# GNN layer kernel, phase B: register loads of eight offsets, no filler products, and row one-hots of two groups in four read back from HBM

## The chip, the cores and the metric

One core of one Trainium2 chip. The metric is the device time of the whole program in microseconds, the median of several runs.

## The reference

Three layers of an attention graph network over 12,500 nodes and 200,000 edges (64 channels), then a residual sum and a layer norm. Cut to what matters:

```python
for l in range(3):
    f1 = relu(x[row] @ nb_W[l] + nb_b[l])
    f2 = relu(x[col] @ self_W[l] + self_b[l])
    h = relu(concatenate([f1, f2], axis=1) @ att1_W[l] + att1_b[l])
    log_alpha = (h @ att2_W[l] + att2_b[l])[:, 0]
    mask = clip(sigmoid(log_alpha) * 1.5 - 0.45, 0.0, 1.0)
    rowsum = segment_sum(mask, row) + 1e-06
    d = clip(rowsum ** (-0.5), 0.0, 10.0)
    vals = mask * d[row] * d[col]
    x = segment_sum(vals[:, None] * x[col], row)
    out = out + x
return layernorm(x_in + out)
```

## The kernel before

Once, at the start, the edges are sorted by the block of 128 nodes that their row lies in, and cut into 1,664 tiles of 128 edges. Eight tiles (U = 8) are a **group**, four groups a **quad**: 208 groups and 52 quads in each layer. Then each layer has three parts: the products over nodes, phase A (the attention mask of every edge, and the sums of the mask over rows), and phase B (the weighted sum of the neighbours' rows).

**Phase A** runs the loop over quads. GpSimd (POOL) gathers the neighbours' rows with 32 indirect DMAs a quad (line 491). VectorE (DVE) makes for each group a one-hot of the edges' rows twice (`hot_a`, `hot_b`, lines 1014 to 1018). The DMA queue of SyncE (SP) stores the gathered rows of groups 0, 1 and 2 of a quad to HBM (`kept_x`), and one-hots over the columns (`look_hot`).

**Phase B** goes over the same quads in its own order. Groups 0, 1 and 2 of a quad are steps 0, 1 and 2, and group 3, whose rows POOL gathers again (line 504), is summed inside step 1. A step works like this:

- TensorE (PE) in `pick_rows` looks up d of the columns for the step after next: 24 bf16 products (line 650) from `look_t` (`onehot_t` in the trace), which SP loads.
- DVE in `look_up` takes the one value that matters of each, eight instructions (line 1078), builds the row one-hot of the next step in f32 with `build_onehot` (line 891), adds the last step's bank to `acc` in `join` (line 1093), and multiplies d with the mask in `weigh` (line 1086).
- ScalarE (ACT) in `scale_rows` multiplies the step's rows by these weights, eight instructions (line 790), and signals after the fourth and the eighth.
- PE clears the step's bank with a product of zeros (line 655) and then in `sum_edges` adds eight f32 products of one-hot and rows (line 517; the trace shows two records for each). Where in the bank a product goes is an offset that is known only at run time. The eight offsets of a group, three bits each, are packed in one 32-bit word of `spots_of`; PE's sequencer loads four such words at the end of a quad (line 663), and cuts an offset out with a shift and a mask ahead of each product.

Behind each step's work PE issues two more products of zeros into bank 7, which nobody reads (`stay_busy(2)`). So a quad has ten products of zeros: four that clear, six that do not.

In the trace the steps are told apart by tile names, since some buffers lie in the space of others: `bank<-k_x,k_hot` is step 0, `bank<-k_x,p_all` step 1, `bank<-onehots,g_hot` group 3, `bank<-p_all,onehots` step 2. PE works through its program in order; its sequencer (PEq) runs ahead of the array where nothing stops it. DVE and ACT are in order as well. The waits on the way of a step: `k_wt` (weights ready, ACT waits), `k_xs` (half of the rows scaled, PE waits), `k_w` (one-hot ready, PE waits), `k_rows` (products of `pick_rows` ready, DVE and SP wait), `k_o` (sums done, DVE and SP wait), `k_acc` (bank free, PE waits). SP issues for each step the load of `look_t` for the step after next and the load of `k_x`.

## Time and profile before

| | us |
|---|---|
| median of 3 runs | 9556.0 (9550.26 to 9559.7) |
| the profiled execution | 9558.15 |
| its span, first to last instruction | 9556.3 |
| phase B, 3 layers (windows 2764:3577, 5728:6540, 8673:9500) | 2452 |

The profile's page gives for each engine the time that it was busy, and for 40 equal slices of the span the busy share in tenths, with the clock that TensorE was granted (10 tenths would be 2.4 GHz, 5 is 1.2 GHz; a 9 stands for 90% or more). Phase B is where PEclk shows 9. The timeline gives instructions in order of time: start, duration, engine, line, operation, output and inputs, count, and in brackets the idle time of the engine before them. Matmuls overlap, so a step of PE is read from start to start. `issue` as releaser means that the profile shows nothing that the engine waited for.

### The profile page before, as it was taken

To read this page: it belongs to the slowest core of one execution; us is meant where nothing else is said; L and a number is where in the kernel's file an instruction comes from. 1 tells how busy PE (TensorE), PEld (TensorE's weight loads), DVE (VectorE), ACT (ScalarE), POOL (GpSimd) and SP (SyncE) were. 2 spreads that over 40 slices of the span, in tenths; PEclk is the share of its full clock that TensorE was granted. 3 is DMA by queue.
4 is the path that set the end of the run, shared out by engine and by line. 5 is a ranking of instruction groups with operands and counts; after the bars stand their busy time and mean duration, and the time that the engine had idled before them with its cause. 6 is when DMAs were issued, how large, how long until landed. Compare 5 with 4: busy or idle time off the path is not lost.

```text
span 9556.3 us, 210132 instructions
## 1 busy us (share of the span) xinstructions
PE 6162.0 (64%) x44565; PEld 5447.6 (57%) x44566; DVE 7276.2 (76%) x29518; ACT 3239.7 (34%) x8192; POOL 6097.4 (64%) x6294
## 2 busy tenths in 40 slices
PE   3145555555569996555555559998555555557997
PEld 1135555555568885555555548887555555556886
DVE  8877777777778887777777778887777777777888
ACT  0022222222235553222222225554222222224554
POOL 0027777777765556777777765555777777775553
PEclk7565555555569996555555559997555555557998
DMA  1014444444454444444444454444444444445443
GB/s 23 0 60 112 111 112 112 112 112 112 112 123 120 119 109 124 111 112 112 112 111 111 111 122 117 120 118 116 111 111 111 111 111 112 112 111 126 119 120 97
DMA packets 986887, 1025.83 MB, mean 107 GB/s; under 512 B 633540, under 2 KB 637412, under 8 KB 986852
## 3 DMA queue, kind: packets, MB, share of 16 engines
q1 hardware_dynamic: 787172, 657.03, 23.2%
q0 software_dynamic: 199680, 368.45, 18.0%
q14 instruction: 28, 0.23, 0.0%
q8 instruction: 7, 0.11, 0.0%
HBM read 744.64 MB, written 280.29 MB: 107 GB/s over the span
## 4 chain that ended last, share of the span: by engine, by line
PE 35%; POOL 23%; issue 20%; DVE 13%; DMA 5%; ACT 3%; ACTq 0%; DVEq 0%; POOLq 0%; SPq 0%
PE bank L517 17%; POOL k_hot L491 10%; POOL g_hot L491 9%; PE bank L650 6%; PE bank L618 6%; DMA k_hot<-qx_table,index 5%; POOL got L491 4%; PE bank L655 3%; DVE acc L903 2%; DVE acc L904 2%; ACT k_x L760 2%; PE bank L608 1%; DVE bank L1034 1%; DVE hidden L1036 1%; DVE small L1039 1%
## 5 line engine op out<-in xcount | busy, mean ns | idle before, releaser
L618 PE MATMUL bank<-p_all,onehot_t 128*128 x10032 | 2301.5, 424 | 1686.5 <-issue 1672.7
L618 PEld LDWEIGHTS bank<-p_all,onehot_t 128*128 128x128 f32 x10032 | 2186.8, 330 | 1737.7 <-issue 1737.7
L491 POOL DMA_INDIRECT got<-qx_table,index x2496 | 2372.0, 950 | 784.3 <-issue 739.5
L504 POOL DMA_INDIRECT got<-y_table,index x1248 | 1330.8, 1066 | 1087.5 <-ACT index L806 658.9
L770 ACT ACTIVATE small<-small 128x8 f32<-128x8 f32 x624 | 130.2, 209 | 3853.6 <-DVE small L1041 3781.4
L491 POOL DMA_INDIRECT k_hot<-qx_table,index x1248 | 1178.0, 944 | 393.5 <-issue 376.0
L491 POOL DMA_INDIRECT g_hot<-qx_table,index x1248 | 1185.4, 950 | 380.4 <-issue 379.2
L517 PE MATMUL bank<-mask,onehots 128*128 128x3 bf16 x4992 | 671.2, 184 | 1041.1 <-DVE mask L1052 1041.1
L517 PEld LDWEIGHTS bank<-mask,onehots 128*128 128x128 bf16 x4992 | 517.4, 104 | 1305.9 <-issue 1200.7
L1078 DVE SCALAR_TENSOR_TENSOR p_all<-iota_b,col_hi,bank 128x104 f32<-128x104 bf16 x3768 | 956.2, 317 | 327.3 <-PE bank L650 322.9
L790 ACT ACTIVATE k_x<-k_x,k_weight 128x64 f32<-128x64 f32 x2496 | 630.0, 334 | 1038.9 <-DVE k_weight L1086 993.4
L1018 DVE TENSOR_SCALAR onehots<-iota_b,rows_now 128x128 bf16<-128x128 bf16 x5040 | 945.6, 280 | 22.4
L1018 DVE TENSOR_SCALAR onehots<-iota_b,rows_b 128x128 bf16<-128x128 bf16 x5016 | 885.5, 272 | 22.0
L755 ACT CAST onehot_t<-bank 128x1024 f32<-128x1024 bf16 x630 | 637.6, 1012 | 524.2 <-PE bank L608 514.7
L1034 DVE TENSOR_TENSOR bank<-bank,got 128x512 f32<-128x512 f32 x312 | 218.2, 699 | 608.9 <-DMA got<-qx_table,index 603.7
L608 PE MATMUL bank<-ident_b,onehots 128*128 128x128 bf16 x5040 | 667.7, 314 | 9.1 <-DVE onehots L1018 9.1
L650 PE MATMUL bank<-d,onehot_t 128*128 128x104 bf16 x11376 | 616.2, 212 | 56.0 <-issue 30.5
L608 PEld LDWEIGHTS bank<-ident_b,onehots 128*128 128x128 bf16 x5040 | 631.7, 164 | 10.3 <-DVE onehots L1018 10.3
L650 PEld LDWEIGHTS bank<-d,onehot_t 128*128 128x128 bf16 x11376 | 546.9, 99 | 80.8 <-issue 61.1
L1036 DVE SCALAR_TENSOR_TENSOR hidden<-bank,a_cur 128x512 f32<-128x512 f32 x624 | 431.3, 691 | 21.4
L655 PE MATMUL bank<-zeros_b 128*128 128x512 bf16 x1563 | 446.2, 384 | 0.0
L1039 DVE TENSOR_REDUCE small<-hidden 128x8 f32<-128x512 f32 x624 | 428.0, 686 | 21.2
(170 smaller groups left out, 9724.3 us busy)
## 6 DMA issues: line engine op xcount, KB each, us to landing
onehot_t<-look_hot SPq DMA_DIRECT2D x474, 256.0 KB, 3.0
k_x<-col_rows SPq DMA_DIRECT2D x318, 256.0 KB
kept_x<-got SPq DMA_DIRECT2D x312, 256.0 KB, 3.2
look_hot<-k_x SPq DMA_DIRECT2D x312, 256.0 KB, 2.1
k_x<-kept_x SPq DMA_DIRECT2D x312, 256.0 KB
look_new<-col_rows SPq DMA_DIRECT2D x156, 256.0 KB
got<-qx_table,index POOLq DMA_INDIRECT x2496
kept_x<-g_hot SPq DMA_DIRECT2D x156, 256.0 KB
```

The lines of the kernel that those rows point to most:

```text
L491: pool.indirect_dma_start(got[j][:, k, :], None, qx_table, bass.IndirectOffsetOnAxis(ap=index[j][:, k:k + 1], axis=0)).then_inc(a_got[j], 16)
L504: pool.indirect_dma_start(got[j][:, k, 0:HID], None, y_table, bass.IndirectOffsetOnAxis(ap=index[j][:, k:k + 1], axis=0)).then_inc(g_got[j ...
L517: return mm(to, lhsT, rhs, start=False, stop=True, skip_group_check=True)
L608: last = turn(bank_t[:, k, :], hot_a[j][:, k, :], ident_b[:, :])
L618: last = mm(bank_p[h][:, k, :], onehot_t[h][:, k, :], p_all[:, ds(ids[k], 1), :].rearrange("p o d -> p (o d)"), start=True, stop=True)
L650: last = mm(bank_d[n % 3][:, e, 0:NB], look_t[i % 3][:, q * (U // 2) + e, :], d3[:, s, :], start=(s == 0), stop=(s == 2))
L655: return mm(to[:, :], zeros_b[:, 0:PARTS], zeros_b[:, :], start=True, stop=True, skip_group_check=True)
L755: a.copy(onehot_t[h][:, :, :], bank_t).then_inc(a_trc, 1)
L790: last = a.activation(to[:, k, 0:HID], rows[:, k, 0:HID], ACT.Copy, scale=by(k))
L1018: last = v.tensor_scalar(to[:, k, :], iota_b[:, :], rows[:, k:k + 1], None, ALU.is_equal)
L1036: link(v.scalar_tensor_tensor(out=hidden[h][:, :, :], in0=bank_p[h], scalar=0.0, in1=a2_cur[:, :].unsqueeze(1).to_broadcast([PARTS, U, HID ...
L1078: last = v.scalar_tensor_tensor(out=picked[:, e, :], in0=iota_b[:, 0:NB], scalar=col_hi[:, ds(at + e, 1)], in1=bank_d[(2 * i + q) % 3][:, ...
```

## The change

Four edits, three of them in phase B:

1. **Offsets.** `spots_of` is gone. PE loads the eight 32-bit offsets of one group straight from `spot_of` (`load_spots`), right behind the sums of the group before. In the product the offset is the register times 64, and shift and mask are gone. The products of the group that comes next use the registers: group order 0, 1, 3, 2 of a quad.
2. **Products of zeros.** `stay_busy` is gone: only the four clearing ones of a quad are left. A bank is cleared before the wait for the one-hot, as before.
3. **Row one-hots of groups 0 and 2 of a quad.** In phase A these lie in `hot_b[0]` in bf16. SP now stores them to HBM (`row_hot`, 256 KB each, two a quad), and DVE waits for that store to land before it overwrites `hot_b[0]`. In phase B SP loads them back (`load_hot`, two a quad, into `hot_in`), and ACT turns them into f32 (`cast_hot`, 128x1024) where DVE built them before. `cast_hot` waits for the load and for the sums that last read `k_hot`. DVE builds only the one-hots of step 1 and of group 3.
4. **Small things.** Two more stores of zeros at the start, one wait of POOL at the start of a layer, and eight small DVE instructions less when the offsets are made.

```diff
@@ (DRAM, SBUF)
+        row_hot = nc.dram_tensor("row_hot", ((2 * QUADS + 1) * PARTS, U * PARTS), BF16, kind="Internal").ap()
...
-        spot_of = sb("spot_of", [1, TILES], I32)
-        spots_of = sb("spots_of", [1, GROUPS + 4], I32)
+        spot_of = sb("spot_of", [1, TILES + U], I32)
...
+        hot_in = {0: look_new[2], 2: sb("hot_in2", [PARTS, U * PARTS], BF16)[:, :]}
...
+        def hot_there(l, quad, i):
+            return l * (QUADS + (i % 3 == 0)) + (quad + (i // 3 + 1))
@@ sync, phase A
                     for j in range(3):
                         load_columns(b, j + 2)
+                        if j != 1:
+                            sp.wait_ge(a_hotb, l * (GROUPS + 1) + (b * 4 + (j + 1)))
+                            sp.sem_inc(sp_go, 1)
+                            sp.dma_start(row_hot[ds((b * 2 + j // 2) * PARTS, PARTS), :],
+                                         hot_b[0].rearrange("p k m -> p (k m)")).then_inc(a_hotst, 16)
                         sp.wait_ge(a_got[j], (l * QUADS + b + 1) * GOT)
@@ sync, phase B
+                def load_hot(b, i):
+                    c = i % 3
+                    if not isinstance(b, int):
+                        sp.wait_ge(k_cast[c], hot_there(l, b, i - 3))
+                        sp.sem_inc(sp_go, 1)
+                    sp.dma_start(hot_in[c], row_hot[ds((b * 2 + (2 * (i // 3) + c // 2)) * PARTS, PARTS), :]).then_inc(k_hotin[c], 16)
...
                         load_look(b * 2, i + 2)
+                        if i % 3 != 2:
+                            load_hot(b * 2, i + 2)
                         sp.wait_ge(*summed(l, b * 2, i - 3))
@@ gpsimd, start of a layer
+                pool.wait_ge(k_cast[0], l * (QUADS + 1))
+                pool.sem_inc(pool_go, 1)
@@ tensor, phase B
-                def stay_busy(n):
-                    for _ in range(n):
-                        clear(bank[7])
-                def spots(b):
-                    pe.load(spot, spots_of[0:1, ds(b * 4, 4)])
-                def sum_edges(to, j, hot, rows, ready, half):
-                    of = pe.snap(spot[j], min_val=0, max_val=(1 << 3 * U) - 1)
-                    to_left = HID.bit_length() - 1
+                def load_spots(g):
+                    pe.load(spot, spot_of[0:1, ds(g * U, U)])
+                def sum_edges(to, hot, rows, there, ready, half, after):
+                    clear(to)
+                    pe.wait_ge(*there)
                     for k in range(U):
-                        bits = of >> (3 * k - to_left) if 3 * k > to_left else of << (to_left - 3 * k) if 3 * k < to_left else of
-                        at = pe.snap(bits & ((U - 1) * HID), min_val=0, max_val=(U - 1) * HID)
+                        at = pe.snap(spot[k], min_val=0, max_val=U - 1)
                         if k % (U // 2) == 0:
                             pe.wait_ge(ready, half + (k // (U // 2) + 1))
-                        last = plus(to[:, ds(at, HID)], hot[:, k, :], rows[:, k, 0:HID])
+                        last = plus(to[:, ds(at * HID, HID)], hot[:, k, :], rows[:, k, 0:HID])
+                    load_spots(after)
...
                         pe.wait_ge(*joined(l, b, i - 3))
-                        clear(bank[i])
-                        pe.wait_ge(k_w, l * (K_STEPS + 1) + k + 1)
-                        sum_edges(bank[i], i, k_hot[i], k_x[i], k_xs, (l * K_STEPS + k) * 2).then_inc(k_o[i], 1)
-                        if i == 2:
-                            spots(b + 1)
+                        there = (k_cast[i], hot_there(l, b, i)) if i != 1 else (k_w, l * QUADS + (b + 1))
+                        sum_edges(bank[i], k_hot[i], k_x[i], there, k_xs, (l * K_STEPS + k) * 2,
+                                  b * 4 + (1, 3, 4)[i]).then_inc(k_o[i], 1)
                         pick_rows(b, i + 2)
                         if i == 1:
                             pe.wait_ge(g_acc, m)
-                            clear(bank[3])
-                            pe.wait_ge(g_w, m + 1)
-                            sum_edges(bank[3], 3, g_hot, g_x, g_xs, m * 2).then_inc(g_o, 1)
-                        stay_busy(2)
+                            sum_edges(bank[3], g_hot, g_x, (g_w, m + 1), g_xs, m * 2, b * 4 + 2).then_inc(g_o, 1)
@@ scalar, phase B
+                def cast_hot(b, i):
+                    act.wait_ge(k_hotin[i % 3], hot_there(l, b, i) * 16)
+                    if not isinstance(b, int):
+                        act.wait_ge(*summed(l, b, i - 3))
+                    a.copy(k_hot[i % 3].rearrange("p k m -> p (k m)"), hot_in[i % 3]).then_inc(k_cast[i % 3], 1)
...
                         scale_rows(k_x[i % 3], k_x[i % 3], lambda k: k_weight[i % 2][:, 1, k:k + 1], k_xs)
+                        if i % 3 == 2:
+                            cast_hot(b * 2, i + 1)
                         if i % 3 != 1:
                             continue
...
                         a.copy(index[j][:, :], col_id[:, ds((b * 8 + (4 * j + 11)) * U, U)]).then_inc(g_idx[j], 1)
+                        cast_hot(b * 2, i + 1)
@@ vector, phase A (build_hot of hot_b[0])
                     dve.wait_ge(*free)
+                    if stored is not None:
+                        dve.wait_ge(a_hotst, stored * 16)
@@ vector, phase B
-                build_onehot(k_hot[0], row_lo[:, 0:U]).then_inc(k_w, 1)
...
                         look_up(i + 1, k + 1, next_at)
-                        build_onehot(k_hot[(i + 1) % 3], row_lo[:, ds(next_at, U)]).then_inc(k_w, 1)
+                        if i % 3 == 0:
+                            build_onehot(k_hot[1], row_lo[:, ds(next_at, U)]).then_inc(k_w, 1)
```

How the rows of PE stand in its program, first before, at the end of the sums of group 3 and the start of those of step 2 (`bank<-p_all,onehots`; rows named L655 are the products of zeros, REGISTER_ALU and ISA are register instructions of the sequencer, some of which carry a wait):

```order
L517 REGISTER_ALU x2
L517 ISA
L517 MATMUL bank<-onehots,g_hot 128x64
L655 MATMUL bank<-zeros_b 128x512 x2
L685 REGISTER_ALU
L655 MATMUL bank<-zeros_b 128x512
L687 ISA
L666 ISA
L517 REGISTER_ALU x2
L517 ISA
L517 MATMUL bank<-p_all,onehots 128x64
```

The same place after the change:

```order
L698 ISA
L550 MATMUL bank<-onehots,g_hot 128x64
L691 ISA
L691 TENSOR_LOAD spot_of
L688 MATMUL bank<-zeros_b 128x512
L698 ISA
L550 ISA
L550 MATMUL bank<-p_all,onehots 128x64
L698 ISA
L550 MATMUL bank<-p_all,onehots 128x64
```

Two of three products of zeros are gone, a load of registers stands between the last product of one group and the first of the next, and one register instruction is left ahead of a product where there were three.

ACT in phase B before, behind the scaling of group 3's rows, until the second step 0 of the loop's body:

```order
L806 ISA
L806 COPY index<-col_id 128x8
L797 REGISTER_ALU
L790 ACTIVATE p_all<-p_all,k_weight 128x64 x8
L796 ISA
L797 REGISTER_ALU
L790 ACTIVATE k_x<-k_x,k_weight 128x64 x8
```

And after:

```order
L846 ISA
L846 COPY index<-col_id 128x8
L824 REGISTER_ALU
L825 CAST onehots<-hot_in 128x1024
L835 REGISTER_ALU
L816 ACTIVATE p_all<-p_all,k_weight 128x64 x8
L822 ISA
L825 CAST k_hot<-look_new 128x1024
L834 ISA
L835 REGISTER_ALU
L816 ACTIVATE k_x<-k_x,k_weight 128x64 x8
```

A cast now stands ahead of the scaling of step 2 and one behind it, ahead of the scaling of step 0.

## Rows read from the trace of the kernel before

**Rows 1.** The page: busy time of the engines, and the granted clock in 40 slices.

```profile
PE 6162.0 (64%) x44565; PEld 5447.6 (57%) x44566; DVE 7276.2 (76%) x29518; ACT 3239.7 (34%) x8192; POOL 6097.4 (64%) x6294
...
PEclk7565555555569996555555559997555555557998
```

**Rows 2.** Lines, 1000:2700 (phase A), POOL: count | busy us, mean ns | idle before.

```profile
L491 POOL DMA_INDIRECT got<-qx_table,index x673 | 636.8, 946 | 205.1 <-issue 192.3 <-ACT index L779 12.8
```

**Rows 3.** Timeline of one quad of phase B: start us, us, what.

```profile
3242.31 2.67 PE L517 MATMUL bank<-k_x,p_all 128*128 128x64 f32 x16 [0.24 <-issue]
...
3244.81 1.27 PE L650 MATMUL bank<-d,onehot_t 128*128 128x104 bf16 x24
...
3245.92 0.38 PE L655 MATMUL bank<-zeros_b 128*128 128x512 bf16 x1
...
3246.14 2.11 PE L517 MATMUL bank<-onehots,g_hot 128*128 128x64 f32 x16
...
3248.09 0.81 PE L655 MATMUL bank<-zeros_b 128*128 128x512 bf16 x3
...
3248.73 2.44 PE L517 MATMUL bank<-p_all,onehots 128*128 128x64 f32 x16
...
3251.36 1.27 PE L650 MATMUL bank<-d,onehot_t 128*128 128x104 bf16 x24 [0.19 <-issue]
3252.34 0.32 DVE L1078 SCALAR_TENSOR_TENSOR p_all<-iota_b,col_hi,bank 128x104 f32<-128x104 bf16 x1 [1.93 <-PE bank L650]
...
3254.30 1.22 DVE L891 TENSOR_TENSOR p_all<-iota_b,row_lo 128x1024 f32<-128x1024 bf16 x1
...
3255.43 0.68 DVE L1093 TENSOR_TENSOR acc<-acc,bank 128x512 f32 x1
...
3256.22 2.02 ACT L790 ACTIVATE k_x<-k_x,k_weight 128x64 f32<-128x64 f32 x8 [4.53 <-DVE k_weight L1086]
...
3257.62 2.62 PE L517 MATMUL bank<-k_x,p_all 128*128 128x64 f32 x16 [0.19 <-issue]
```

**Rows 4.** Timeline of PE, start of the first phase B: clock 0.5, then 1.0.

```profile
2770.49 3.67 PE L517 MATMUL bank<-k_x,k_hot 128*128 128x64 f32 x16 [4.19 <-ACT k_x L790]
2773.95 2.29 PE L650 MATMUL bank<-d,onehot_t 128*128 128x104 bf16 x24
2776.03 1.48 PE L655 MATMUL bank<-zeros_b 128*128 128x512 bf16 x3
2777.31 1.98 PE L517 MATMUL bank<-k_x,p_all 128*128 128x64 f32 x16
2779.13 1.26 PE L650 MATMUL bank<-d,onehot_t 128*128 128x104 bf16 x24
```

**Rows 5.** Register loads of PE by line: count, duration ns min/median/max.

```profile
L663 PEldq TENSOR_LOAD <-spots_of x159: 328/332/761, 2764.3 to 9496.7; - x159
...
L613 PEldq TENSOR_LOAD <-block_of x627: 1917/1922/2570, 673.8 to 8665.5; - x157
```

**Rows 6.** Page, a cast by ACT; POOL in 3000:3500; a DMA of 256 KB.

```profile
L755 ACT CAST onehot_t<-bank 128x1024 f32<-128x1024 bf16 x630 | 637.6, 1012 | 524.2 <-PE bank L608 514.7
...
L504 POOL DMA_INDIRECT got<-y_table,index x263 | 280.3, 1066 | 225.0 <-ACT index L806 151.1 <-issue 74.0
...
onehot_t<-look_hot SPq DMA_DIRECT2D x474, 256.0 KB, 3.0
```

**Rows 7.** Timeline of PE where the clock fell, and where it did not.

```profile
3549.85 2.75 PE L517 MATMUL bank<-k_x,p_all 128*128 128x64 f32 x16 [0.51 <-ACT k_x L790]
3552.39 2.29 PE L650 MATMUL bank<-d,onehot_t 128*128 128x104 bf16 x24
...
9488.02 2.62 PE L517 MATMUL bank<-k_x,p_all 128*128 128x64 f32 x16 [0.19 <-issue]
9490.52 1.27 PE L650 MATMUL bank<-d,onehot_t 128*128 128x104 bf16 x24
```

**Rows 8.** Windows: busy us (instructions) of PE PEld DVE ACT POOL, clock, DMA share, GB/s.

```profile
3552.00:3556.00 4.00, 4.00 (x36) 3.90 (x36) 3.64 (x20) 2.49 (x11) 0.00 (x0) 0.57 0.14 34
```

More of the change, by code:

```diff
@@ L964, in _ @@
             spots = spot_of[0:1, 0:TILES].rearrange("p (t k) -> p t k", k=U)
-            link(v.tensor_tensor(spots, by_step, by_step[:, :, 0:1].to_broadcast(steps_wide), ALU.subtract))
-            v.memset(spots_of[0:1, GROUPS:GROUPS + 4], 0)
-            packed = spots_of[0:1, 0:GROUPS].unsqueeze(2)
-            link(v.tensor_copy(packed, spots[:, :, U - 1:U]))
-            for k in reversed(range(U - 1)):
-                last = v.scalar_tensor_tensor(out=packed, in0=packed, scalar=8.0, in1=spots[:, :, k:k + 1],
-                                              op0=ALU.mult, op1=ALU.add)
-                if k:
-                    link(last)
-            last.then_inc(s_edges, 1)
+            v.memset(spot_of[0:1, TILES:TILES + U], 0)
+            v.tensor_tensor(spots, by_step, by_step[:, :, 0:1].to_broadcast(steps_wide), ALU.subtract).then_inc(s_edges, 1)
             dve.wait_ge(s_edges, 1)
```

28 lines of the change are left out of this document (20 added, 8 removed).

## The prediction

> **What bounds the kernel now.** I read the page first: DVE is busy for 76% of the span, PE and POOL for 64%, and no engine is at its limit over the whole [rows 1]. The clock line splits the program: PEclk is 5 for long stretches (phase A) and 9 in three short ones (phase B) [rows 1]. So each stage needs its own reading.
>
> In phase A POOL gathers without a break: one gather is 946 ns of work and some 0.3 us of idle time ahead of it (205.1 us over 673), which is 1.25 us [rows 2]. 32 of them make 40 us a quad, 52 quads 2.08 ms, and three layers 6.2 ms of the 9.56. PE, DVE and ACT wait for gathers there.
>
> In phase B PE is busy all the time, and nearly each row of PE in the timeline follows the last with no idle time [rows 3]. A quad is the stretch from the sums of step 1 to the same sums one quad later, 3242.31 to 3257.62, 15.3 us. 156 such quads are 2.39 ms, nearly all of phase B. The reader is to follow one loop through it, in which each piece starts when the last ends: sums of step 1 2.50, `pick_rows` 1.11, a product of zeros 0.22, sums of group 3 1.95, three products of zeros 0.64, sums of step 2 2.63 (0.19 of it idle), the first half of `pick_rows` and the way to DVE 0.98, eight look-ups 1.96, a one-hot 1.13, join and weights 0.79, scaling until PE starts 1.40. That is 15.31 us [rows 3]. Step 0 of PE lies beside it.
>
> **The change, part by part.**
>
> *Sums.* The sixteen records of one `sum_edges` take 2.50 us from start to start where PE's sequencer works through shift, mask and address ahead of each product [rows 3], and 1.82 us (2777.31 to 2779.13) at the same clock right after a slow stretch, when products had piled up ahead of the array [rows 4]. The difference of 0.68 us is the price of the register instructions, and with one of three left the sequencer is no longer the slower of the two. In the loop are the sums of step 1 (2.50 to 1.82), of group 3 (1.95 to 1.82) and of step 2 (2.44 to 1.82): 1.43 us less. From the fourth scaled row to the first product 1.40 us pass, of which two of three register instructions go: 0.2 us less.
>
> *Products of zeros.* In the loop three stand behind group 3, and one is left: 0.64 to 0.22, 0.42 us less. The others (two behind step 0, two behind step 2) lie beside DVE's part of the loop and are worth nothing here; the clock is their other side, below.
>
> *The load of eight offsets.* The trace has two register loads: four 32-bit words in 332 ns, and eight 16-bit numbers in 1922 ns [rows 5]. The bounds for eight 32-bit words are 0.33 us (as for four) and 1.92 us. I take 0.45 us, near the 332 ns, since type and tensor are the same as there; twice 332 is 0.66. It blocks the sequencer, not the array, and products already handed over cover it: with two of three register instructions gone, the sequencer needs for 1.82 us of array work at most half of its 2.50 us. Where the wait for the second half of the rows ends late (2.02 us of scaling [rows 3]) the cover is thinner. For three loads in the loop I take 0.4 us exposed in all, against the 0.19 us of idle time behind step 2 now: 0.2 us more. At 0.66 us each it is 0.6 us more on top, 100 us of the total.
>
> *One-hots from HBM.* DVE loses two of four one-hots, 2.27 us a quad, but not the one that stands in the loop (3254.30, step 1's) [rows 3]. DVE waits 1.93 us in a quad already [rows 3], so these two only widen a gap: worth nothing to this loop. ACT gets two casts. The same shape out of PSUM takes 1.01 us [rows 6]. ACT works 4 x 2.02 + 0.18 us a quad and waits for the rest, so 10.3 us of 13.7 is no bound. But one cast stands ahead of the scaling of step 2, and the sums of step 2 wait for it. There PE has pick, clear and sums of group 3 to do, which covers the cast. SP gets two more loads of 256 KB, and its queue has for each a wait on a cast, behind which the loads of `k_x` and of the next `look_t` stand. They land some 3 us after issue [rows 6] and are needed a step or more later: nothing, as long as that holds.
>
> *Phase A.* Two stores of 256 KB a quad, with one wait each on SP, and a wait of DVE for the landing before `hot_b[0]` is used again, two groups (some 20 us) later. Behind SP's wait stand the stores of `kept_x`. POOL sets the pace, with indices ready about a group ahead: 0, at most 10 us in all (the first and last quads of a layer).
>
> *The sum.* 1.43 + 0.2 + 0.42 - 0.2 = 1.85 us less by these rows. I take off 0.2 us for what becomes late next (the waits between the engines that now show, DVE's own register loads behind a missing one-hot): 1.65 us a quad, 13.7 us instead of 15.3. Times 156 it is 257 us. Against the profiled execution's 9558 us that gives 9301, and 9299 against the median, 2 us below.
>
> **The clock.** With the clock at 1.2 GHz the sums of a group take 3.46 us (2770.49 to 2773.95) and `pick_rows` 2.08 [rows 4], so each group costs 1.64 and each pick 0.97 us more than at 2.4 GHz. Phase B keeps the high clock almost without a break, but at 3549.85 PE idled 0.51 us, did the sums of step 1, and the `pick_rows` behind them ran at the low clock: 2.29 us instead of 1.27, mean clock 0.57 in that stretch [rows 7, 8]. With an idle time of 0.19 us in the same place, at 9488.02, it did not fall [rows 7]. It came back within 4 us, with pick and three products of zeros close together at the start of a phase [rows 4].
>
> After the change PE has less to do in a quad, and I expect about 0.9 us of idle time ahead of the sums of step 1: from the sums of step 2 to those of step 1 the loop takes 8.0 us by the sum above, and PE's work in it is 2 x (1.82 + 1.11 + 0.22) = 6.3 us and some 0.8 for loads and the loop's end (an allowance). That is more idle time than what let the clock fall once, and the six products that kept PE busy are gone. That a fall needs the right moment is my reading of the rows (0.51 us is seen with a fall, 0.19 without). I take one fall in ten quads, 16 in all, a guess. One lasts longer than before, since no three products of zeros follow a pick; a whole quad at the low clock costs 3 x 1.64 + 1.5 x 0.97 + 0.4 = 6.8 us in the loop, and I take 5 us for a fall. 16 x 5 = 80 us.
>
> The Trainium skill (TensorE: Matmul & The Clock Gate, "Loop structure matters more than you think") holds that matmuls back to back keep the engine warm and that it is a long wait between them which lets it go cold. By that alone no idle time of a microsecond would matter, and the time would be the 9299 of the first rival. The trace speaks against it with the fall behind 0.51 us.
>
> **Forecast:** 9556 - 257 + 80 = 9379, say 9380 us; as a case 9340 to 9450. Chance 0.45.
>
> **Rivals.**
>
> *The clock holds throughout.* Then the 80 us stay: 9300 us, 9285 to 9340. For it speaks that sums get denser as well, and that a quad of 13.7 us may meet no bad moment. Chance 0.25.
>
> *The clock falls often.* The place is the idle time ahead of the sums of step 1; the price 5 us a fall; it decides from 257 / 5 = 51 falls, one in three quads. In every second quad it is 78 falls: 9556 - 257 + 390 = 9689 us, slower than before. For it speaks that the idle time comes back in each quad and that a cold stretch needs PE to be packed densely to end, for which the filler products served. Chance 0.15, the half of it on the slower side (9450 to 9750).
>
> *The load costs as much as the one of `block_of`*, 1.92 us [rows 5]. Each of three in the loop is then 1.47 us longer than I took: 4.4 us, less the 1.65 gained, is 2.75 us a quad, 429 us, or 9985 us. It decides from 0.45 + 1.65 / 3 = 1.0 us a load. Against it speak the 332 ns for the same tensor type. Chance 0.05.
>
> The Trainium skill (Runtime: NRT & Kernel Launch, "Instruction fetch mechanics") puts such a load at about 200 ns a register, even in bulk. For eight that would be an estimate of 1.6 us, which agrees with the 1922 ns for eight 16-bit numbers and not with the 332 ns for four 32-bit words. By it the last rival would come out, somewhat milder.
>
> *The gain goes elsewhere.* The casts, SP's queue with its new waits, or the loads of `k_x` under 30% more traffic become the loop, and it stays at 15 us and more: 9520 to 9570 us. Against it: POOL's eight gathers take 8 x (1.07 + 0.3) = 10.9 us a quad and it waits 4.6 for ACT (151.1 us in 33 quads) [rows 6]; ACT (10.3 us) and DVE (15.3 - 1.93 - 2.27 = 11.1 us) have room too. Chance 0.10.
>
> **How the numbers follow.** A measurement of this kernel tells 0.2%, 19 us, from no change. Faster by more: 0.45 + 0.25, 0.05 of the often-falling clock, 0.02 of the last: 0.77. Within: 0.02 and 0.07: 0.09. Slower: 0.08 + 0.05 + 0.01: 0.14. The range for 8 in 10 is 9285 to 9560; left out are the slower cases, and a little below.
>
> **What would show it.** In the changed profile: sixteen records of sums in 1.8 to 2.0 us; a register load of `spot_of` near 0.45 us; a quad of 13.7 us where the clock is 1.0; DVE's waits for PE longer than 1.93 us; phase A unchanged at 1.25 us a gather. The mean clock in phase B tells the first cases apart: near 1.0 now, about 0.95 by the forecast, under 0.85 where falls eat the gain. Wrong it would be with a load over 1 us, a quad over 14.5 us at full clock, or POOL with waits in phase A.

## The result, and the profile after

The changed kernel takes 9282.7 us (median of 4, 9279.9 to 9284.6) against 9555.7 for the kernel before: 0.971 of its time (95% interval 0.970 to 0.973). That is 273 us less, where 176 were forecast, and 2 us below the low end of the range. The profiled execution took 9279.89 us.

The page of the changed kernel:

```profile
PE 5731.3 (62%) x43629; PEld 5187.9 (56%) x43630; DVE 6885.6 (74%) x29195; ACT 3520.0 (38%) x8507; POOL 6079.3 (66%) x6294
...
PEclk7565555555559996555555558998555555556998
```

The pattern of [rows 1] is there again, with slightly shorter stretches of 9. Phase A's gathers, in 1000:2700, POOL (columns as in [rows 2]):

```profile
L524 POOL DMA_INDIRECT got<-qx_table,index x677 | 639.6, 945 | 206.3 <-issue 205.4 <-ACT index L805 0.9
```

945 ns of work and 0.3 us of idle time ahead, as in [rows 2]: the two stores per quad cost nothing there. From the first to the last gather, the three phases A took 2084, 2086 and 2087 us, before 2088, 2089 and 2089. From the first to the last sums, phase B took 716, 716 and 715 us, before 804, 805 and 803. So 265 us of the gain lie in phase B and 9 in phase A.

One quad of phase B in the timeline, PE only, to be laid beside [rows 3] (L550 the sums, L683 `pick_rows`, L688 a product of zeros):

```profile
3223.78 2.06 PE L550 MATMUL bank<-k_x,p_all 128*128 128x64 f32 x16 [0.81 <-ACT k_x L816]
3226.21 1.27 PE L683 MATMUL bank<-d,onehot_t 128*128 128x104 bf16 x24 [0.37 <-issue]
3227.32 0.38 PE L688 MATMUL bank<-zeros_b 128*128 128x512 bf16 x1
3227.53 1.90 PE L550 MATMUL bank<-onehots,g_hot 128*128 128x64 f32 x16
3229.27 0.38 PE L688 MATMUL bank<-zeros_b 128*128 128x512 bf16 x1
3229.48 1.89 PE L550 MATMUL bank<-p_all,onehots 128*128 128x64 f32 x16
3231.21 1.26 PE L683 MATMUL bank<-d,onehot_t 128*128 128x104 bf16 x24
...
3237.29 2.06 PE L550 MATMUL bank<-k_x,p_all 128*128 128x64 f32 x16 [0.64 <-ACT k_x L816]
```

And DVE and ACT in the part of the loop that is theirs, first DVE and then ACT:

```profile
3232.20 0.32 DVE L1116 SCALAR_TENSOR_TENSOR p_all<-iota_b,col_hi,bank 128x104 f32<-128x104 bf16 x1 [1.14 <-PE bank L683]
...
3234.16 1.22 DVE L932 TENSOR_TENSOR p_all<-iota_b,row_lo 128x1024 f32<-128x1024 bf16 x1
3235.30 0.68 DVE L1131 TENSOR_TENSOR acc<-acc,bank 128x512 f32 x1
```

```profile
3236.08 2.02 ACT L816 ACTIVATE k_x<-k_x,k_weight 128x64 f32<-128x64 f32 x8 [2.57 <-DVE k_weight L1124]
```

Read from start to start, the same chain as in [rows 3] closes after 13.51 us:

| piece | before | after |
|---|---|---|
| sums of step 1, its load | 2.50 | 2.43 |
| pick_rows | 1.11 | 1.11 |
| product of zeros | 0.22 | 0.21 |
| sums of group 3, its load | 1.95 | 1.74 |
| products of zeros | 0.64 | 0.21 |
| sums of step 2, its load | 2.63 | 1.73 |
| half of pick, way to DVE | 0.98 | 0.99 |
| look-ups | 1.96 | 1.96 |
| one-hot | 1.13 | 1.14 |
| join, weights | 0.79 | 0.78 |
| scaling, until PE starts | 1.40 | 1.21 |
| **quad** | 15.31 | 13.51 |

The 2.43 us of step 1 are 2.06 of sums and 0.37 in which PE is idle behind them and the profile names only `issue`: its sequencer is loading registers. The load, by line (count, ns min/median/max):

```profile
L691 PEldq TENSOR_LOAD <-spot_of x627: 587/591/1722, 2756.0 to 9217.9; - x157
```

What the engines waited for in 3000:3400 (us in total, times, longest):

```profile
POOL got L537 <- ACT index L846: 81.3, 27, 4.7
...
DVE p_all L1116 <- PE bank L683: 63.2, 59, 1.9
...
ACT k_x L816 <- DMA k_x<-kept_x: 31.9, 29, 1.6
...
DVE acc L1131 <- issue: 13.0, 27, 0.5
```

ACT now waits for a load of `k_x` once a quad, which it did not before. That is step 0's scaling, which lies beside the loop (0.81 us of slack ahead of the sums of step 1 are left). The windows of the same stretch show the clock (columns as in [rows 8]):

```profile
3000.00:3400.00 400.00, 357.35 (x4115) 332.08 (x4112) 323.22 (x1673) 286.98 (x1022) 251.16 (x236) 0.98 0.57 174
```

Over the whole trace I counted quads (starts of the sums of step 1) by the granted clock in them. Before: 148 of 153 quads inside the phases at 1.0 throughout, 15.37 us each. After: 128 at 1.0 throughout, 13.50 us each, and 25 that touch a stretch at 0.5, 15.17 us each; there are 20 such falls. One of them, where PE idled ahead of step 1:

```profile
3304.82 2.06 PE L550 MATMUL bank<-k_x,p_all 128*128 128x64 f32 x16 [0.71 <-ACT k_x L816]
3307.25 2.23 PE L683 MATMUL bank<-d,onehot_t 128*128 128x104 bf16 x24 [0.37 <-issue]
3309.27 0.63 PE L688 MATMUL bank<-zeros_b 128*128 128x512 bf16 x1
3309.70 2.40 PE L550 MATMUL bank<-onehots,g_hot 128*128 128x64 f32 x16
3311.93 0.38 PE L688 MATMUL bank<-zeros_b 128*128 128x512 bf16 x1
3312.15 1.89 PE L550 MATMUL bank<-p_all,onehots 128*128 128x64 f32 x16
```

`pick_rows` takes 2.02 us from start to start instead of 1.11, the product of zeros 0.43 instead of 0.21, the sums behind it 2.23 instead of 1.74, and then the clock is back. This fall cost 0.91, 0.22 and 0.49 us, together 1.6 us, where the prediction had put 5 us on one. Of the 20 falls, 12 follow an idle time ahead of the sums of step 1 (0.64 to 1.19 us), 5 one ahead of the sums of step 0 (0.41 to 0.75 us), and 3 stand at the start of a phase, as in the kernel before.

### The profile page after: what moved, and what is told of

The parts are those of the page before. It is cut to its first block, busy times and chain, and to the rows that moved or that the text cites. A ratio compares the mean times of both kernels' runs of the same rounds, so it can differ in the third digit from the quotient of the medians.

```text
span 9278.1 us, 202668 instructions
## 1 busy us (share of the span) xinstructions
PE 5731.3 (62%) x43629; PEld 5187.9 (56%) x43630; DVE 6885.6 (74%) x29195; ACT 3520.0 (38%) x8507; POOL 6079.3 (66%) x6294
## 4 chain that ended last, share of the span: by engine, by line
POOL 43%; issue 24%; PE 17%; DVE 10%; ACT 2%; DVEq 2%; DMA 1%; ACTq 0%; POOLq 0%; SPq 0%
POOL got L524 22%; POOL k_hot L524 11%; POOL g_hot L524 10%; PE bank L550 10%; PE bank L683 3%; DVE acc L944 2%; DVE acc L945 2%; DVE p_all L1116 2%; ACT k_x L816 1%; PE bank L651 1%; DVE acc L1131 1%; PE bank L688 1%; PE bank L608 1%; PE bank L599 1%; PE bank L574 1%
## 5 line engine op out<-in xcount | busy, mean ns | idle before, releaser
L550 PE MATMUL bank<-mask,onehots 128*128 128x3 bf16 x4992 | 669.4, 185 | 967.0 <-DVE mask L1089 967.0
L1116 DVE SCALAR_TENSOR_TENSOR p_all<-iota_b,col_hi,bank 128x104 f32<-128x104 bf16 x3768 | 953.4, 316 | 358.7 <-PE bank L683 350.4
L550 PEld LDWEIGHTS bank<-mask,onehots 128*128 128x128 bf16 x4992 | 518.2, 105 | 1228.8 <-issue 1126.2
L1054 DVE TENSOR_SCALAR onehots<-iota_b,rows_now 128x128 bf16<-128x128 bf16 x5040 | 900.0, 283 | 23.0
L683 PE MATMUL bank<-d,onehot_t 128*128 128x104 bf16 x11376 | 632.2, 215 | 132.8 <-issue 105.3
L683 PEld LDWEIGHTS bank<-d,onehot_t 128*128 128x128 bf16 x11376 | 578.1, 102 | 172.6 <-issue 156.6
L1131 DVE TENSOR_TENSOR acc<-acc,bank 128x512 f32 x627 | 426.6, 680 | 87.9 <-issue 67.7
```

The costliest lines, as they stand in the source:

```text
L550: return mm(to, lhsT, rhs, start=False, stop=True, skip_group_check=True)
L683: last = mm(bank_d[n % 3][:, e, 0:NB], look_t[i % 3][:, q * (U // 2) + e, :], d3[:, s, :], start=(s == 0), stop=(s == 2))
L1054: last = v.tensor_scalar(to[:, k, :], iota_b[:, :], rows[:, k:k + 1], None, ALU.is_equal)
L1116: last = v.scalar_tensor_tensor(out=picked[:, e, :], in0=iota_b[:, 0:NB], scalar=col_hi[:, ds(at + e, 1)], in1=bank_d[(2 * i + q) % 3][:, ...
L1131: return v.tensor_tensor(some, some, sums[:, :], ALU.add)
```

## The experiments

**Theory A** is the prediction's mechanism: the loop gets shorter by the register instructions and by two products of zeros behind group 3, and the one-hots by way of HBM are worth nothing. **Theory B** holds that without its three products of zeros PE idles and the clock takes the gain back. The first four kernels take the change apart. Their kernel before took 9565.5 us on that chip.

**Only the products of zeros left out** (kernel before):

```diff
                         pick_rows(b, i + 2)
...
-                        stay_busy(2)
```

> The kernel before without its six idle products of zeros a quad, nothing else changed. Theory A (the sum of the prediction): two of them stand in the loop behind group 3, so 0.42 us a quad less, 65 us in all: 9490 us, with a few falls of the clock at 1.3 us each on top. Theory B (the register instructions ahead of the products hide them: the sequencer needs the 0.42 us anyway to get ready for the sums of step 2): no gain in the loop, and with more idle time of TensorE the clock falls more often than with the filler: 9556 to 9620 us, mean clock of phase B under 0.97.

Measured: 9591.4 us, 1.0027 (1.0016 to 1.0037). A quad at full clock is 15.38 us, the same as before. 85 falls are seen in place of 5, but the quads with one are only 0.46 us longer. The two products in the loop were no gain here, since without them PE's sequencer still works through its register instructions before the array gets the next product. The timeline of PE:

```profile
3234.34 2.16 PE L517 MATMUL bank<-onehots,g_hot 128*128 128x64 f32 x16
3236.34 0.38 PE L655 MATMUL bank<-zeros_b 128*128 128x512 bf16 x1
3236.76 2.65 PE L517 MATMUL bank<-p_all,onehots 128*128 128x64 f32 x16
```

From the sums of group 3 to those of step 2 it is 2.42 us, not 2.59, since one product of zeros stands between and not three, but the next sums start 0.42 us behind it, not 0.22. From those to the pick (3239.59) it is then 2.83 us, not 2.63. Together 5.25 us against 5.22: the time of the products came back as waiting for the sequencer. Theory B is right for this kernel: the time lies in its range, and the mean clock of the first phase B is 0.93, against 0.99 before.

**The change with its products of zeros back:**

```diff
                             sum_edges(bank[3], g_hot, g_x, (g_w, m + 1), g_xs, m * 2, b * 4 + 2).then_inc(g_o, 1)
+                        stay_busy(2)
```

> The changed kernel with the six idle products of zeros a quad put back behind each step. Theory A (two of the six lengthen the loop by 0.42 us a quad, 65 us; the falls of the clock, some 20 at 1.3 us, go away, 26 us): 9283 + 65 - 26 = 9320 us, no stretch of low clock inside phase B. Theory B (what the filler costs in the loop is covered by the register load of 0.59 us that stands there now): 9283 - 26 = 9257 us.

Measured: 9370.2 us, 0.9798 (0.9781 to 0.9814). A full-clock quad is 13.95 us, 0.45 more than after: this is the term of 0.42 us, now that the sequencer no longer hides it. The products do not hold the clock up in this kernel: there are 24 falls, about as many as without them (20), while in the kernel before they do (5 falls with them, 85 without). One:

```profile
3228.31 2.06 PE L550 MATMUL bank<-k_x,p_all 128*128 128x64 f32 x16 [0.60 <-ACT k_x L822]
3230.74 1.87 PE L683 MATMUL bank<-d,onehot_t 128*128 128x104 bf16 x24 [0.37 <-issue]
3232.41 0.63 PE L688 MATMUL bank<-zeros_b 128*128 128x512 bf16 x1
3232.83 2.76 PE L550 MATMUL bank<-onehots,g_hot 128*128 128x64 f32 x16
```

Three products of zeros stood right ahead of the first row, and 0.60 us of idle time are left between. So taking the products out is worth 0.84% of the time before (0.9714 against 0.9798), some 80 us, on top of the other edits, and costs 26 us alone. One edit's worth depends on the other.

**The offsets alone** (kernel before with `load_spots` and the registers as they come; products of zeros and DVE's one-hots stay):

```diff
-                        at = pe.snap(bits & ((U - 1) * HID), min_val=0, max_val=(U - 1) * HID)
+                        at = pe.snap(spot[k], min_val=0, max_val=U - 1)
...
-                        last = plus(to[:, ds(at, HID)], hot[:, k, :], rows[:, k, 0:HID])
+                        last = plus(to[:, ds(at * HID, HID)], hot[:, k, :], rows[:, k, 0:HID])
+                    load_spots(after)
```

> The kernel before with only the edit of the offsets (eight 32-bit words a load behind each group's sums; no shift and mask), filler products and all one-hots on VectorE kept. Theory A (the register instructions are what the loop gains from): a quad goes from 15.4 to about 14.0 us, limited below by VectorE's own 13.4 us: 9330 to 9370 us. Theory B (the one-hots are what counts, the sums only move waits about): 9500 to 9556 us.

Measured: 9373.1 us, 0.9797 (0.9780 to 0.9813), 13.92 us a full-clock quad (1.45 less than before), 24 falls. It differs from the run above only in the one-hots, and the two agree within 3 us. As theory A has it.

```profile
3234.54 2.06 PE L516 MATMUL bank<-k_x,p_all 128*128 128x64 f32 x16 [0.57 <-ACT k_x L786]
3236.98 1.27 PE L649 MATMUL bank<-d,onehot_t 128*128 128x104 bf16 x24 [0.37 <-issue]
3238.08 0.38 PE L654 MATMUL bank<-zeros_b 128*128 128x512 bf16 x1
3238.30 1.89 PE L516 MATMUL bank<-onehots,g_hot 128*128 128x64 f32 x16
3240.03 0.81 PE L654 MATMUL bank<-zeros_b 128*128 128x512 bf16 x3
```

**The one-hots from HBM alone** (the changed kernel with the packed offsets, three register instructions and `stay_busy(2)` of before):

```diff
-                        at = pe.snap(spot[k], min_val=0, max_val=U - 1)
+                        bits = of >> (3 * k - to_left) if 3 * k > to_left else of << (to_left - 3 * k) if 3 * k < to_left else of
+                        at = pe.snap(bits & ((U - 1) * HID), min_val=0, max_val=(U - 1) * HID)
...
+                        stay_busy(2)
```

> The kernel before with only the one-hots of groups 0 and 2 of a quad through HBM and ScalarE; packed offsets with shift and mask, and the filler products, kept. Theory A (these two one-hots lie beside the loop, and VectorE waited 1.9 us a quad already): no change, 9540 to 9560 us, with VectorE waiting over 4 us a quad for TensorE. Theory B (VectorE was the bound): 2.27 us a quad less, 9200 us; half of it 9380 us.

Measured: 9551.9 us, 0.9984 (0.9975 to 0.9994): 14 us less, which is no change by the bound of 0.2%. It is the sum of two small effects in the trace: a full-clock quad is 15.19 us, 0.19 less than before (some 29 us in all), and 38 falls stand in place of 5 (30 us instead of 15). Neither was tried by itself. DVE's time went into its wait, in 3000:3400:

```profile
DVE p_all L1133 <- PE bank L684: 93.9, 51, 2.6
...
ACT k_x L825 <- DMA k_x<-kept_x: 29.1, 26, 1.9
```

The second row shows that the wait of ACT for `k_x` comes with these edits, and the time shows no cost of it.

**Are the falls due to the idle time, and what do they cost?** The next kernels ran on another chip (kernel before: 9552.0 us there). First, the changed kernel with three idle products behind step 0 only, beside the loop, where PE waits anyway:

```diff
+                        if i == 0:
+                            stay_busy(3)
```

> The kernel of e5_filler_step0 again, since the chip of that run needed 13002 us for the kernel before and VectorE had idle times there that the other chips do not show. Three idle products of zeros behind the look-up products of step 0 only. Theory A: the falls of the clock behind the sums of step 1 go, 33 us less than the changed kernel: 9250 us. Theory B: 9283 us or more.

Measured: 9264.7 us, 0.9700 (0.9684 to 0.9716), 18 us below the changed kernel on the same chip. 6 falls are left of the 18 in the trace of the changed kernel from this chip (the next run), and a full-clock quad is 13.51 us, as without them. None of those ahead of step 1 is left. The idle time ahead of step 1 is filled:

```profile
3234.24 1.03 PE L688 MATMUL bank<-zeros_b 128*128 128x512 bf16 x4
3235.28 2.06 PE L550 MATMUL bank<-k_x,p_all 128*128 128x64 f32 x16
```

So most falls do hang on that idle time, and 12 fewer falls gave 18 us, 1.5 us each. They do not hang on it alone: 0.64 us of idle time and more stand ahead of step 1 in 116 of the 156 quads of the changed kernel (median of all 0.75), and 12 have a fall there. What picks the quad stays open.

A kernel meant to load the offsets twice:

```diff
                     load_spots(after)
+                    load_spots(after)
```

> The kernel of e6_double_load again, for the same reason. Two register loads behind each group's sums. Theory A (exposed in full behind step 1, in part behind group 3 and step 2): 1.0 to 1.6 us more a quad, 9440 to 9530 us. Theory B (hidden as the first mostly is): under 9345 us.

Only one load was left in its program (the trace has 627, as after), so it was the changed kernel once more: 9282.9 us, 0.9719 (0.9702 to 0.9735). It tells nothing of a load, but is the value on this chip against which these runs are read.

**The changed kernel with all one-hots built by DVE** (no `row_hot`, no casts):

```diff
-                        if i % 3 == 0:
-                            build_onehot(k_hot[1], row_lo[:, ds(next_at, U)]).then_inc(k_w, 1)
+                        build_onehot(k_hot[(i + 1) % 3], row_lo[:, ds(next_at, U)]).then_inc(k_w, 1)
```

> The kernel of e7_offsets_no_filler again, for the same reason: the changed kernel with all one-hots built by VectorE. Theory A (they lie beside the loop): 9283 to 9300 us. Theory B (VectorE's 13.4 us of work a quad bound a loop of 13.5): 9300 to 9380 us. On the disturbed chip it was slower than the changed kernel's relatives, 1.0048 of before, which fits B where VectorE is the slow engine.

Measured: 9286.0 us, 0.9721 (0.9705 to 0.9737), 3 us beside the changed kernel, 13.53 us a full-clock quad, 15 falls. The third edit is worth nothing with the short loop either.

**The one-hot of step 1 ahead of the look-ups.** The loop's table says what is left on it that need not be: DVE builds the one-hot (1.14 us) between look-ups and weights, although it waits 1.14 us for PE just before and the sums of step 1 need that one-hot only later.

```diff
-                        look_up(i + 1, k + 1, next_at)
                         if i % 3 == 0:
                             build_onehot(k_hot[1], row_lo[:, ds(next_at, U)]).then_inc(k_w, 1)
+                        look_up(i + 1, k + 1, next_at)
```

> The kernel of e9_onehot_first again, for the same reason: step 1's one-hot ahead of the look-ups. Theory A (the loop is the one of the prediction): 12.4 us a quad, 9100 to 9140 us, hardly a fall of the clock. Theory B (another loop of nearly the same length): 9250 to 9283 us. The few quads at full clock of the first run had a mean of 12.44 us, against 13.48 and 13.5 in the two kernels with the old order, which speaks for A.

Measured: 9092.8 us, 0.9517 (0.9501 to 0.9533): 190 us below the changed kernel on the same chip, and faster than both. A full-clock quad is 12.39 us, 1.11 less, which is the one-hot. 1.11 x 156 = 173 us; the rest goes with falls, 6 in place of 18. The phases B took 653, 652 and 652 us. DVE and then PE there:

```profile
3232.43 1.23 DVE L932 TENSOR_TENSOR g_hot<-iota_b,row_lo 128x1024 f32<-128x1024 bf16 x1
3233.57 0.32 DVE L1116 SCALAR_TENSOR_TENSOR p_all<-iota_b,col_hi,bank 128x104 f32<-128x104 bf16 x1
```

```profile
3232.50 1.27 PE L683 MATMUL bank<-d,onehot_t 128*128 128x104 bf16 x24 [0.40 <-issue]
3233.61 0.38 PE L688 MATMUL bank<-zeros_b 128*128 128x512 bf16 x1
3233.82 1.90 PE L550 MATMUL bank<-k_x,p_all 128*128 128x64 f32 x16
```

The sums of step 1 follow the product of zeros without idle time. PE is busy 375.7 us of 400 in this window, DVE 356.3, with the clock at 1.00 throughout:

```profile
3000.00:3400.00 400.00, 375.72 (x4486) 357.03 (x4484) 356.28 (x1835) 314.93 (x1121) 278.15 (x260) 1.00 0.65 189
```

**A dearer load.** The changed kernel with `spot_of` in 16 bits, so that eight offsets load as `block_of` does:

```diff
-        spot_of = sb("spot_of", [1, TILES + U], I32)
+        spot_of = sb("spot_of", [1, TILES + U], mybir.dt.int16)
```

> The changed kernel with spot_of in 16-bit words, nothing else changed, so that a register load of eight offsets should take about 1.92 us as that of block_of does, and not 0.59. Theory A (a load stands in the loop in full, as the prediction's rival had it): 3 x 1.33 = 4.0 us more a quad, 9900 us. Theory B (products already handed over cover about a microsecond of a load behind group 3 and step 2, and only step 1's stands there in full): 1.33 + 2 x 0.5 to 1.0 = 2.3 to 3.3 us a quad, 9640 to 9800 us. Theory C (covered for the most part): under 9500 us.

On the two chips where it ran the kernel before took 12831 and 12978 us, and not some 9556. In this kernel's traces from there the mean granted clock in phase B is 0.67 to 0.69, and DVE stands idle between its own instructions. Ratios from these chips can't be turned into microseconds of the others. Measured: 1.0087 (1.0070 to 1.0104). On the second chip:

> The kernel of e13_short_offsets again, since VectorE had idle times on the chip of that run that the other chips do not show. Register loads of 1.92 us instead of 0.59. Theory A (each of three stands in the loop in full): 9900 us. Theory B (a microsecond or less of two of them is covered): 9640 to 9800 us. Theory C (covered for the most part): under 9500 us.

Measured: 1.0170 (1.0152 to 1.0189). What can be read is local to PE. The load:

```profile
L691 PEldq TENSOR_LOAD <-spot_of x627: 1917/1921/3290, 3547.3 to 13141.5; - x157
```

And a sum of step 1 at full clock, with what follows:

```profile
3623.64 2.06 PE L550 MATMUL bank<-k_x,p_all 128*128 128x64 f32 x16
3627.40 1.84 PE L683 MATMUL bank<-d,onehot_t 128*128 128x104 bf16 x24 [1.70 <-issue]
```

1.70 us idle, where the changed kernel has 0.37: the load's 1.33 us more come through in full behind step 1. Over all places at full clock, from the last record of sums to the next instruction (median, first chip's trace): behind step 1 1.97 us against 0.65, behind step 2 1.55 against 0.11, behind group 3, until the sums of step 2, 1.21 against 0.33. The places behind step 1 are of two kinds. Where the clock had been high and the sums took 1.78 us, since their rows came while they ran, it is 1.97 us in each (13 of 21 places, and 16 of 50 on the second chip). Where PE had just come out of a low stretch and the sums took 1.62 us, it is 0.39 to 0.69 us (the other 8 and 34): products had piled up there and covered some 1.4 us of the load. So by an estimate from the first kind a load of 1.92 us would be some 3.6 us dearer a quad in a loop at full clock, more than theory B's 2.3 to 3.3, and one of 0.59 us is covered wholly behind group 3 and step 2, where the sums took 1.62 us as well. How long the whole program would take with it on a chip of 9556 us was not measured.

**The other runs on such chips.** All one-hots by DVE, step 1's ahead of the look-ups, with the offsets as in the change and no idle products, should tell whether the one-hots from HBM pay in the shorter loop:

```diff
+                        if i % 3 == 0:
+                            build_onehot(k_hot[(i + 1) % 3], row_lo[:, ds(next_at, U)]).then_inc(k_w, 1)
                         look_up(i + 1, k + 1, next_at)
-                        build_onehot(k_hot[(i + 1) % 3], row_lo[:, ds(next_at, U)]).then_inc(k_w, 1)
+                        if i % 3 != 0:
+                            build_onehot(k_hot[(i + 1) % 3], row_lo[:, ds(next_at, U)]).then_inc(k_w, 1)
```

> e9_again's kernel with all one-hots built by VectorE and no detour through HBM: the kernel before with the edits of the offsets and the filler, and step 1's one-hot ahead of the look-ups. Theory A (VectorE's 13.4 us a quad take over from the loop of 12.4): 13.4 to 13.6 us a quad, 9250 to 9285 us, so that the one-hots from HBM are worth a microsecond a quad only in the shorter loop. Theory B (they are worth nothing there too): 9090 to 9110 us.

Measured: 0.9843 (0.9826 to 0.9859). On the second chip:

> The kernel of e12_offsets_onehot_first again, for the same reason. Theory A (VectorE's 13.4 us a quad take over): 9250 to 9285 us. Theory B (the one-hots through HBM are worth nothing in the shorter loop either): 9090 to 9110 us.

Measured: 0.9811 (0.9784 to 0.9837). The kernel before with this edit and nothing else:

> The kernel before with only step 1's one-hot built ahead of the look-ups. Theory A (the loop of the prediction is that of the kernel before): 1.1 us less, 15.4 to 14.3 us a quad: 9380 to 9400 us. Theory B (TensorE's sequencer with its shifts and masks, filler included, binds by itself near 15 us): 9500 us or more.

Measured: 0.9949 (0.9932 to 0.9965), faster even with its own offsets. Six quads of its trace are at full clock throughout, and the three of them in which DVE never waits for `remote` (below), each the last quad of its phase, took 14.17 to 14.19 us. The quads of the kernel before take 15.37, so this agrees with theory A's 14.3. The kernel of 9092.8 us with `k_x` loaded ahead of the one-hots (SP):

```diff
                         load_look(b * 2, i + 2)
-                        if i % 3 != 2:
-                            load_hot(b * 2, i + 2)
...
+                        if i % 3 != 2:
+                            load_hot(b * 2, i + 2)
```

> e9_again's kernel with the load of k_x issued ahead of the load of the one-hot on SyncE's queue, so that it does not stand behind the wait for a cast. ScalarE waits 1.2 us a quad for k_x in e9_again. Theory A (that wait is in no loop): within 10 us of 9093. Theory B (it is part of the loop of 12.4 us): 0.3 to 1 us less a quad, 8940 to 9045 us.

Measured: 0.9932 (0.9915 to 0.9948).

Four kernels told of above had first run on a third such chip (before: 13002 us). The one with idle products behind step 0:

> The changed kernel with three idle products of zeros (0.65 us) behind the look-up products of step 0, where TensorE idles 0.81 us ahead of the sums of step 1, and nowhere else. Theory A (a fall of the clock needs that idle time, and costs 1.67 us a quad that it strikes): the stretches of low clock behind the sums of step 1 go, 20 of them, 33 us less: 9250 us at full effect, the full-clock quad stays 13.5 us. Theory B (the falls have another cause, or the filler delays the sums of step 1): 9283 us or more.

Measured: 0.9989 (0.9979 to 0.9999). The changed kernel itself, meant with two loads:

> The changed kernel with the register load of eight offsets issued twice behind each group's sums; it prices a load. One is 0.59 us and, in the loop, 0.37 us of idle time stand behind the sums of step 1 now, none behind the other two. Theory A (exposed in full behind step 1, in part behind group 3 and step 2): 1.0 to 1.6 us more a quad, 160 to 250 us: 9440 to 9530 us. Theory B (the second load hides as the first mostly does): under 0.4 us a quad, under 9345 us.

Measured: 0.9967 (0.9955 to 0.9978). All one-hots by DVE:

> The kernel before with the edits of the offsets and of the filler, and all one-hots still built by VectorE: what the detour through HBM and ScalarE is worth once the other two are in. Theory A (nothing, since these one-hots lie beside the loop): 9283 to 9300 us. Theory B (VectorE's 13.4 us of work a quad bound a loop of 13.5 us, so that each delay shows): 20 to 100 us slower than the changed kernel, 9300 to 9380 us.

Measured: 1.0048 (1.0031 to 1.0065). The one-hot ahead of the look-ups:

> The changed kernel with the one one-hot that stands in the loop, step 1's, built ahead of the look-ups, in the 1.1 us in which VectorE waits for TensorE, and not behind them. Theory A (the loop is the one of the prediction): 1.13 us of it go, the quad falls from 13.5 to 12.4 us or to what comes next (VectorE 11.1 us, POOL 10.9 us a quad), 9100 to 9140 us, and with TensorE's idle time ahead of step 1 the falls of the clock. Theory B (another loop of nearly the same length binds, such as the loads of k_x that ScalarE waits for): 9250 to 9283 us.

Measured: 0.9942 (0.9925 to 0.9958). The change that is worth 2.8% elsewhere is worth 0.3% there, and the one worth 4.8% is worth 0.6%. Two things in these traces bear on that. At the low clock the sums of group 3 take 3.31 us from start to start with the packed offsets as with the loaded ones (2.00 and 1.73 at full clock), so the change shortens nothing there. And DVE idles for 109 to 157 us of 3700:4100 in phase B with `remote` as releaser, that is with no work of this core named, up to 9.3 us at a time. No trace of the other chips shows that. The few quads at full clock are as long as on the other chips (12.38 to 12.51 us with the one-hot ahead of the look-ups, 13.46 to 13.51 without it), but for one of 12.79 us. The kernel with all one-hots by DVE has four, of 12.47, 13.06, 13.30 and 13.31 us: a hint of theory A. On the chip where both ran it took 12628 us and the one with `k_x` ahead 12735 us, which points the other way. So whether the one-hots from HBM begin to pay in the shorter loop, and what the order alone saves the whole kernel before, stays open for a chip of 9556 us.

## Why the prediction was right and wrong, point by point

- **Sums, loads, products of zeros and address instructions: right, and near exact, in part by luck.** The sums with their loads were to fall from 7.08 to 3 x 1.82 + 0.4 = 5.86 us and measure 5.90, in which two misses cancel: sums whose rows lie ready take 1.73 us, not 1.82, but step 1's take some 0.15 us more since their rows come late, and its load shows more than was allowed; products of zeros 0.64 to 0.22, measured 0.21; scaling until PE starts 1.40 to 1.20, measured 1.21. The sum by rows, 1.85 us a quad, measured 1.87 over all full-clock quads (15.37 to 13.50).
- **The load: mis-sized, with little effect.** 0.45 us were taken, 0.59 measured, and 0.53 us of one load show in place of 0.4 of three: 0.65 us to the next instruction behind step 1, against 0.11 behind group 3 and step 2, where it is hidden. The prediction had said that cover is thinner where the wait for the second half of the rows ends late. Step 1 is such a place (ACT scales its rows while PE sums), group 3 and step 2 are not. No run took that cause by itself, but the 16-bit loads show it: behind step 1 they cost 1.97 us where the rows came late and 0.39 to 0.69 us where products had piled up.
- **The allowance of 0.2 us for what is late next: not needed.** It is 0.2 x 156 = 31 us of the 97 us between forecast and result, and 3 more are the 0.02 us by which the sum was low. PE's pieces got shorter in a loop in which each waits for the last, and nothing else was near.
- **The price of a fall: the step that failed.** Forecast: 16 falls of 5 us, 80 us. Measured: the 25 quads with low clock are 1.67 us longer, 42 us; the 5 of before were 3.09 us longer (18.46 us against 15.37), 15 us, mostly at the start of a phase. So the 15 falls that came new cost 26 us, 1.8 us each. Place (ahead of step 1 for 12 of the 20) and number were near, the number by a guess, as the prediction says; the price was about three times too high. It was taken from 6.8 us, a whole quad at the low clock, though the fall of [rows 7, 8] held just the pick. That row alone gives 2.29 - 1.27 = 1.0 us and what follows in the same stretch. A fall was also to last longer without three products of zeros behind a pick: most low stretches last 3.4 us with them (24 falls) and without (20).
- **The 97 us close:** 31 + 3 for the loop, 80 - 26 = 54 for the clock, 9 for phase A, which was allowed 0 to 10 us more and took 9 less. Why it did was not tried; in the traces of the kernels near 9556 us and below, a phase A takes 2085 to 2093 us, so 3 us each is within what they differ by.
- **The one-hots from HBM: right, within 0.2%.** Three pairs of kernels say so: alone 0.9984, with the offsets 9370.2 against 9373.1 us, without the products of zeros 9282.9 against 9286.0.
- **The rivals.** The one with a clock that holds (9285 to 9340 us, 0.25) is the nearest in time, but not in mechanism, since the clock did fall. That the clock takes the gain back is refuted by both count and price: it wanted 51 falls at 5 us to decide and 78 for its 9689 us, and there were 20 at some 2 us. Its reason, that a cold stretch needs the filler products to end, did not hold either. A load of 1.92 us was the right price for 16-bit words only. SP's queue did become later (ACT waits 1.1 us for `k_x` once a quad), as the fourth rival had it, but beside the loop.
- **What the signs showed.** Sixteen records of sums in 1.89 to 2.06 us, foreseen 1.8 to 2.0; quad 13.5 for 13.7; phase A's gathers unchanged; mean clock of phase B 0.97 for 0.95. One sign failed in part: DVE's wait in the loop fell to 1.14 us, where over 1.93 was foreseen. Its free time went into a second wait for PE (59 in 29.6 quads, 63.2 us, so 2.1 us a quad in two waits), behind the steps whose one-hot it no longer builds.

## What to carry to other kernels

Write the loop down as a table from start to start, and read what an edit is worth from that; then look in the same table for a piece that stands behind a wait and could stand ahead of it. Here that find, one line moved, was worth 190 us, more than two thirds of the whole change. An edit that hides behind another (products of zeros behind register instructions) measures nothing or worse alone, so try it again after the other is made. Price a clock fall from how long it lasts in the trace, not from what a stretch at the low clock costs.

## What the runs showed of the hardware

- On PE the time of a register load went with the count and the type of the words: four 32-bit words 332 ns, eight 591 ns, eight 16-bit numbers 1921 ns (the last two from the same tensor at the same place, with another type). Twice as many words cost 1.8 times as much, and the short type 3.3 times. The Trainium skill (Runtime: NRT & Kernel Launch, "Instruction fetch mechanics") puts a load at about 200 ns a register; that is near the 16-bit load (240 ns) and not the 32-bit ones (74 to 83 ns).
- Falls of TensorE's clock from 2.4 to 1.2 GHz inside a phase were seen in the changed kernel behind 0.4 to 1.2 us of idle time followed by a group of f32 sums (17 of 20), and all of these were over within 4 us. Most quads with such an idle time have no fall. Three products of zeros in the idle time ahead of step 1 took away every fall there. The new falls cost 1.8 us each in the changed kernel, and a quad with one was only 0.5 us longer in the kernel before without its idle products (85 falls). That the register instructions pace PE there anyway is a likely reason, not one that was tried.
- On three chips the kernel before took 12,831 to 13,002 us, and the other versions 12,628 to 13,200, at a mean granted clock of 0.67 to 0.79 in phase B. In the kernel with 16-bit offsets, in 3700:4100, DVE waited 134.7 us in 17 stretches of up to 8.6 us for `p_all L1116 <- remote`. What slows DVE there is open.
